# Self-attention on one core: one projection job per head slot, every hand-over between engines one slot later, and the stacked q/k parts moved by group of four heads

## The reference, cut to what matters

```python
def _L0_attn_ref(x, w_qkv, w_out):
    b, s, _ = x.shape
    qkv = (x @ w_qkv).reshape(b, s, 3, HEADS, HEAD_DIM)
    q, k, v = (qkv[:, :, 0], qkv[:, :, 1], qkv[:, :, 2])
    q = q / scale
    scores = jnp.einsum('bqhd,bkhd->bhqk', q, k)
    scores = jnp.where(causal_mask[None, None], scores, NEG)
    attn = jax.nn.softmax(scores, axis=-1)
    out = jnp.einsum('bhqk,bkhd->bqhd', attn, v).reshape(b, s, HIDDEN)
    return out @ w_out
x = x + _L0_attn_ref(_layernorm(x), L0_attn_w_qkv, L0_attn_w_out)
x = x + _L0_xattn_ref(_layernorm(x), ctx_2048, ...)
x = x + _L0_ffn_ref(_layernorm(x), ...)
```

## Time and profile before

| | us |
|---|---|
| median of 3 runs | 863.87 |
| lowest, highest | 860.68, 865.61 |
| profiled execution | 868.03 |
| its span, first to last instruction | 866.3 |
| PE busy in the span | 762.7 |
| DVE, ACT, POOL busy | 529.1, 370.4, 312.2 |

### The profile page before, as it was taken

How to read it: one execution, slowest core, us unless ns; L and a number is a source line. 1 busy time by engine, 2 the same in 40 slices (tenths; PEclk the granted TensorE clock), 3 DMA queues, 4 the chain that set the end, 5 groups by cost and what they waited for, 6 DMA issues and landing times. The chain is left out here.

```text
span 866.3 us, 19948 instructions
## 1 busy us (share of the span) xinstructions
PE 762.7 (88%) x6424; PEld 688.1 (79%) x6425; DVE 529.1 (61%) x1557; ACT 370.4 (43%) x1145; POOL 312.2 (36%) x456
## 2 busy tenths in 40 slices
PE   4798989898989999757999999999999985739995
PEld 4787979888888888646899998989899974637884
DVE  4678685868686867546565655556464533834664
ACT  4476675757575767534423232313133220622221
POOL 3376574757565656641000101010101101124662
PEclk9999999999999999879999999999999997868998
DMA  9643343444444434306712425060502111765630
GB/s 345 147 114 94 105 101 106 93 118 93 116 93 118 93 94 115 101 1 208 286 52 72 99 23 113 8 121 20 101 30 67 59 15 49 168 163 152 199 122 24
DMA packets 49575, 90.90 MB, mean 105 GB/s; under 512 B 11390, under 2 KB 11518, under 8 KB 49408
## 3 DMA queue, kind: packets, MB, share of 16 engines
q1 hardware_dynamic: 43872, 77.80, 34.2%
q0 software_dynamic: 5664, 12.61, 4.7%
HBM read 51.95 MB, written 18.77 MB: 82 GB/s over the span
## 5 line engine op out<-in xcount | busy, mean ns | idle before, releaser
L398 ACT ACTIVATE prob<-prob,nmax 128x128 f32<-128x128 f32 (+1 forms) x256 | 114.5, 448 | 77.9 <-DVE nmax L576 77.9
L337 POOL TENSOR_TENSOR pt_part<-pt_rest,pt_part 128x384 bf16<-128x384 f32 x128 | 117.8, 921 | 10.2
L335 POOL CAST pt_part<-pt_rest 128x384 bf16<-128x384 f32 x128 | 67.4, 527 | 113.5 <-DVE pt_rest L585 112.1
L576 DVE CUSTOM_DVE_ANT_0 prob<-a_s,mask 128x128 f32<-128x128 f32 (+1 forms) x256 | 80.2, 350 | 4.1 <-PE a_s L457 3.2
L585 DVE TENSOR_TENSOR pt_rest<-a_t,pt_part 128x384 f32<-128x384 f32 x128 | 70.8, 553 | 7.2 <-ACT pt_part L408 7.0
L408 ACT CAST pt_part<-a_t 128x384 bf16<-128x384 f32 x128 | 60.6, 473 | 32.3 <-PE a_t L470 32.1
L470 PE MATMUL a_t<-ident,prob 128*128 128x128 f32 x384 | 63.5, 275 | 12.2 <-DVE pt_rest L585 11.8
L457 PE MATMUL a_s<-stack 96*128 96x256 f32 x256 | 61.8, 324 | 0.2 <-DVE nmax L576 0.2
L470 PEld LDWEIGHTS a_t<-ident,prob 128*128 128x128 f32 x384 | 45.2, 141 | 17.9 <-issue 15.3
L488 PE MATMUL a_o<-pt_part,v_part 128*32 128x256 bf16 (+1 forms) x1536 | 40.4, 258 | 14.2 <-POOL pt_part L337 13.9
L922 ACT CAST b_kt_hi<-b_bank 128x256 fp32r<-128x256 f32 (+1 forms) x48 | 20.5, 445 | 66.1 <-PE b_bank L56 65.2
(11 more groups left out here) (217 smaller groups left out, 1986.1 us busy)
## 6 DMA issues: line engine op xcount, KB each, us to landing
stack<-qk SPq DMA_DIRECT2D x192, 128.0 KB, 2.4
stage<-in_w SPq DMA_DIRECT2D x8, 1024.0 KB, 8.9
xin<-in_x SPq DMA_DIRECT2D x8, 512.0 KB, 3.6
xr<-in_x SPq DMA_DIRECT2D x8, 512.0 KB, 3.6
x<-xr SPq DMA_DIRECT2D x8, 512.0 KB, 2.8
xin<-x SPq DMA_DIRECT2D x8, 512.0 KB, 8.9
b_cin<-in_ctx SPq DMA_DIRECT2D x8, 512.0 KB, 3.5
xr<-x SPq DMA_DIRECT2D x8, 512.0 KB
```

The lines of the kernel that those rows point to most:

```text
L335: nc.gpsimd.tensor_copy(pt_part[1][:, t % NPT, :], rest).then_inc(pt_mid_done, 1)
L337: nc.gpsimd.tensor_tensor(pt_part[2][:, t % NPT, :], rest, pt_part[1][:, t % NPT, :], ALU.subtract).then_inc(pt_done, 1)
L398: a = nc.scalar.activation(prob[:, e % NPROB, cols], prob[:, e % NPROB, cols], ACT.Exp, scale=-1.0, bias=nmax[:, e, q:q + 1], accum_out=rs ...
L576: m = nc.vector.tensor_tensor_reduce(out=prob[:, s % NPROB, cols], in0=s_ps[s % 2][:, q, 0:P * (q + 1)], in1=mask[:, P * (1 - q):], scale= ...
```

## The change

**Jobs.** The table has one job in every slot. u0 and u1 are made in their own batch, in slots 2 and 3, and no longer in the prologue and in slots 12 and 13 of the batch before. k3 goes from slot 2 to 1, X0 and X1 from 5 and 6 to 6 and 7, y0 and y1 from 7 and 8 to 8 and 9.

**Hand-overs.** ACT now writes a job's hi part in the slot after the job, as its first work, and DVE writes the lo part in that slot behind the scores of the head. PE does the transposes ahead of the values and the job. On ACT the exponentials go last. The copy of the transposed reciprocals and the copy of the scaled output go one slot later. The norm is stretched: statistics in slot 0, aggregation in 2, reciprocal root in 3, application in 4. `r_sb` and `o_sb` have memory of their own.

**Stack.** It moves by group of four heads: 12 DMAs of 64 KB for each of four groups, each group after its own k job, with one semaphore; PE waits for all 12 at a group's first head.

The diff, cut to what the prediction speaks of:

```diff
-        SLOTS = {0: ["q3"], 2: ["k3"], 4: ["w0"], 5: ["w1", "X0"], 6: ["X1"], 7: ["y0"], 8: ["y1"], 9: ["q0"], 10: ["k0"],
-                 11: ["q1", "k1"], 12: ["u0"], 13: ["u1"], 14: ["q2"], 15: ["k2"]}
+        SLOTS = {0: ["q3"], 1: ["k3"], 2: ["u0"], 3: ["u1"], 4: ["w0"], 5: ["w1"], 6: ["X0"], 7: ["X1"], 8: ["y0"],
+                 9: ["y1"], 10: ["q0"], 11: ["k0"], 12: ["q1"], 13: ["k1"], 14: ["q2"], 15: ["k2"]}
-        PROLOGUE = ["X0", "X1", "q0", "k0", "q1", "k1", "q2", "k2", "u0", "u1"]
+        PROLOGUE = ["X0", "X1", "q0", "k0", "q1", "k1", "q2", "k2"]
-        EPILOGUE_SLOTS = 10
+        EPILOGUE_SLOTS = 11
+        STATS_AT, AGGR_AT, RSTD_AT, APPLY_AT = 0, 2, 3, 4
...
-            def stack_half(half):
+            def stack_group(g, n, early):
+
+                wait(sp, job_ev, job_at(f"k{g}", n) + 1)
+                sp.sem_inc(tick_sp, 1)
+                wait(sp, s_done, early)
                 for j in range(HG):
                     for r, parts in enumerate((slice(0, 3, 2), slice(1, 3), slice(0, 4, 3))):
-                        dst = stack[HD * r:HD * (r + 1), half, j, :, :, :].bitcast(F32)
-                        src = qk[HD * j:HD * (j + 1), half, parts, :, :].bitcast(F32)
-                        sp.dma_start(dst.rearrange("p w g s -> p w (g s)"),
-                                     src.rearrange("p w g s -> p w (g s)")).then_inc(stacked[half][j], 16)
+                        sp.dma_start(stack[HD * r:HD * (r + 1), g, j, :, :].bitcast(F32),
+                                     qk[HD * j:HD * (j + 1), g // GH, parts, g % GH, :].bitcast(F32))\
+                            .then_inc(stacked[g], 16)
...
+                stack_group(2, n - 1, n * H - HG)
...
-                wait(sp, s_done, n * H)
-                stack_half(1)
+                stack_group(3, n, n * H)
...
                 if has("k1", n):
-                    wait(sp, job_ev, job_at("k1", n) + 1)
-                    sp.sem_inc(tick_sp, 1)
-                    wait(sp, s_done, n * H + H // 2)
-                    stack_half(0)
+                    stack_group(0, n, n * H + HG)
+                    stack_group(1, n, n * H + 2 * HG)
...
             def slot(n, h):
+                for j, of in jobs_before(h, n):
+                    if j not in LATE:
+                        evac(j, of)
+                g = group_at(h, ON_LAG, n)
+                if g is not None:
+                    act.wait_ge(r_done, groups_before(h, ON_LAG, n) + 1)
+                    wait(act, on_done, groups_before(h, ON_LAG, n))
+                    nc.scalar.copy(r_sb[:], o_ps[g % 2][:, 1, :]).then_inc(rs_done, 1)
...
-                    if s % (H // 2) < HG:
-                        pe.wait_ge(stacked[g // GH][j], (n + 1) * HEAD_IN)
+                    if j == 0:
+                        pe.wait_ge(stacked[g], (n + 1) * GROUP_IN)
...
-                g = group_at(h, AV_LAG, n)
-                if g is not None:
-                    heads_by_values(g, h, n)
-                for j in jobs_of(h, n):
-                    job(j, n)
                 t = head_at(h, T_LAG, n)
...
+                g = group_at(h, AV_LAG, n)
+                if g is not None:
+                    heads_by_values(g, h, n)
+                for j in jobs_of(h, n):
+                    job(j, n)
...
-                if head_at(h, 0, n) is not None and (not isinstance(n, int) or n < B - 1):
-                    if h == 0:
-                        norm_stats(n + 1)
-                    if h == 2:
-                        norm_apply(n + 1)
+                if norm_at(h, STATS_AT, n):
+                    norm_stats(n + 1)
+                if norm_at(h, AGGR_AT, n):
+                    norm_aggr(n + 1)
+                if norm_at(h, APPLY_AT, n):
+                    norm_apply(n + 1)
```

More of the change, by code:

```diff
@@ L119, in self_attention @@
         job_done, job_hi, job_ev = sem("a_job_done"), sem("a_job_hi"), sem("a_job_ev")
-        stacked = [[sem(f"stacked_{half}_{j}") for j in range(HG)] for half in range(2)]
+        stacked = [sem(f"stacked{g}") for g in range(G)]
         s_done, mx_done, ex_done = sem("s_done"), sem("mx_done"), sem("ex_done")
@@ L179, in jobs_of, with jobs_before, norm_at @@
             return [j for j in SLOTS.get(slot, []) if has(j, n)]
+        def jobs_before(slot, n):
+            t = slot - JOB_LAG
+            if t >= 0:
+                return [(j, n) for j in jobs_of(t, n)]
+            if isinstance(n, int) and n == 0:
+                return []
+            return [(j, n - 1) for j in jobs_of(H + t, n - 1 if isinstance(n, int) else n)]
+        def norm_at(slot, at, n):
+            return slot == at and (not isinstance(n, int) or n < B - 1)
         def head_at(slot, lag, n):
@@ L327, in slot @@
             def slot(n, h):
[L328 removed]
+                if norm_at(h, RSTD_AT, n):
                     next_rstd(n + 1)
@@ L338, in slot @@
                                             ALU.subtract).then_inc(pt_done, 1)
-                before = h - LO_JOB_LAG
-                for j in jobs_of(before, n) if before >= 0 else jobs_of(H + before, n - 1 if isinstance(n, int) else n):
-                    of = n if before >= 0 else n - 1
-                    if j[0] in "uw" and not (isinstance(of, int) and of < 0):
+                for j, of in jobs_before(h, n):
+                    if j[0] in "uw":
                         v_lower_parts(j, of)
@@ L580, in slot @@
                     m.then_inc(mx_done, 1)
+                for j, of in jobs_before(h, n):
+                    if j in LATE:
+                        dve.wait_ge(job_done, job_at(j, of) + 1)
+                        dve.wait_ge(xr_in, 16 * of)
+                        xt = xr[:, int(j[1]), :]
+                        nc.vector.tensor_tensor(xt, bank(j, of)[:, :], xt, ALU.add).then_inc(job_ev, 1)
+                    else:
+                        evac(j, of)
                 t = head_at(h, LO_LAG, n)
```

102 lines of the change are left out of this document (41 added, 61 removed).

## The result

The changed kernel takes 874.33 us (median of 19 runs, 871.2 to 878.09), the kernel before, on the same chip, 866.17 us (19 runs, 860.48 to 871.51). The ratio is 1.0095, with a 95% interval of 1.0078 to 1.0113: it is slower by about 8 us, or 1%. Forecast was 865, that is 1 us more than the 863.87 which the kernel before had then; of the 9.3 us between 865 and 874.33, 2.3 are that the kernel before has a median of 866.17 here.

What follows compares the result with a forecast made beforehand. PE was taken as the bound: 39.2 us of work in a 44.13 us batch, the rest waits. 863.87 + 0 (six steady batches) + 1 (first) + 0.3 (last) = 865 us; 8-in-10 range 855 to 873.

Steps and rivals of the forecast that it cites:

- the gain of 1.7 us a batch by the hand-overs: Steady batch: PE's lost time falls from 4.9 to 3.2 us, as waits for POOL and uncopied jobs go; error 1 us.
- the net of zero for six batches: Steady batches: the hand-overs' gain is given back at the stack, so each stays at 44.1 us.
- waits for DVE at slots 4, 7, 8: PE waits for DVE's `pt_rest` at the transposes of these slots: 0.8, 0.95 and 1.45 us a batch.
- PE's work without waits: Steady batch: the same matmuls as before, so PE's 39.2 us stay.
- the running sum: DVE's work added up against PE's slot starts, 16.4 us in eight slots of 17.3, to place and size PE's waits.
- The stack's wait: Slot 16 (slot 0 of the next batch): PE waits 1.7 to 1.8 us for group 0's twelve DMAs, issued 0.64 apart.
- First batch, +1 forecast: First scores 0.6 us earlier, but v jobs in slots 2 and 3 and a new stack wait: +1, bounds 0 and +4.
- The term for the v jobs: First batch: two v jobs, 2.8 us, leave the prologue for slots 2 and 3, where DVE half hides them.
- Last batch, +0.3 forecast: Its own u0 and u1, 2.8 us, fill slots where PE waits for DVE anyway: +0.3, bounds 0 and +2.8.
- A: Rival: half-size stack DMAs issue in about 0.4 us, so no stack wait; six batches gain 1.7 each, 855 us; chance 0.22.
- C: Rival: the three DVE waits vanish too and only the stack wait remains, 843 us; chance 0.06.
- B: Rival: the clock falls around the X-only slots in all six steady batches instead of one, 872.5 us; chance 0.2.

Runs made afterwards that it cites:

- e1: Changed kernel, but PE waits at each stacked head for its own three DMAs instead of twelve at a group's first head; 859.0 us, ratio 0.9945.
- e9: Changed kernel with waits by head, the norm two batches ahead, and x loaded ahead of the bursts of groups 2 and 3; 866.31 us, ratio 0.9976.
- e11: Changed kernel with waits by head and another job table (both X jobs in slot 8 with values), norm in slots 4, 5 and 7; 845.11 us, ratio 0.9735.
- e2: Changed kernel with u0 and u1 of the first batch alone back in the prologue; 873.63 us, ratio 1.0111.
- e10: Changed kernel with waits by head and u0 and u1 of the last batch left out; 862.1 us, ratio 0.9932.
- e7: Changed kernel with waits by head and PE's jobs ahead of its transposes, as in the kernel before; 866.84 us, ratio 1.0008.

## Why the prediction was wrong

**The step that failed most is the gain of 1.7 us a batch by the hand-overs**, and with it the net of zero for six batches. e1 has the change without the group's wait, and its steady batch is 43.80 us where before has 44.13: 0.3 gained. The stack takes 1.04 (44.84 less 43.80), so a steady batch is 0.7 longer rather than equal. The places of the waits were right, their sizes were not. By the starts in PE's timeline (scores to transposes, less the 0.24 of a slot without a wait), in the forecast's terms:

| a steady batch, us | forecast | measured |
|---|---|---|
| waits for DVE at slots 4, 7, 8 | 0.8, 0.95, 1.45 | 1.05, 1.00, 1.7 |
| small ones at slots 11 and 12 | 0 | 0.45 |
| the stack | 1.7 | 1.1 |
| PE's work without waits | 39.2 | about 39.5 |
| the kernel before: waits, work | 4.9, 39.2 | about 4.7, 39.4 |

e9 and e11 show that the causes of the three waits are those of the running sum: the aggregation in slot 2, and slots that hold only an X job. Slot 4's miss of 0.25 has a reason in the trace. I took 0.58 us for the aggregation in its new place, and it takes 0.86 (213.10 to 213.96), because its last instruction, `a_veps`, takes 0.59 us there (at 213.46), with POOL at work beside it, where before it took 0.17 (at 204.22). Why slot 8's wait is 0.2 longer, and where the small ones come from, stays open. PE's work was nearly the same in both orders, as I had it.

**The stack's wait** was right in its place, its cause and the issue time (0.64 forecast, 0.66 measured). Counted from the start of slot 12 (193.54), group 0 is there after 10.95 us instead of 11.3, since a DMA lands after 2.0 us and not 2.4, and PE is ready for it after 9.9 instead of 9.5: 1.1 instead of 1.7 to 1.8.

**First batch, +1 forecast, +3.0 measured** (the second batch's first scores at 67.45 instead of 64.43). The start is right: 0.6 forecast, 0.8 won (28.48 for 29.26). The wait at slot 16 is 2.1 instead of 1.7. The term for the v jobs had no ground: two leave slots 12 and 13 of this batch as two come into slots 2 and 3, so b0 has as many jobs as before. What makes up the rest isn't in the sum at all: the two falls of the clock, 3 us, where before has none in b0. So b0 is 3.8 longer: 2.1 and 3.0, less 1.3 that the rest gains. e1, which doesn't stand 4.2 us ahead of its first scores, has one of the two falls and starts its second batch at 61.53. That the wait brings the fall fits this, but of the eight waits for the stack over a microsecond in the changed kernel and e2 only four have a fall right behind them, so it is not shown.

**Last batch, +0.3 forecast, +2.5 measured.** No wait for the stack lies in it; I split it ahead of slot 10, in the kernel before, in e1 and in the changed kernel:

```profile
331.77:359.81 28.04, 24.48 (x283) 21.54 (x281) 16.90 (x66) 16.40 (x60) 17.92 (x27) 0.94 0.32 79
359.81:393.72 33.91, 20.66 (x217) 16.21 (x216) 15.79 (x54) 12.73 (x45) 14.60 (x21) 0.80 0.09 32
```
```profile
325.77:355.62 29.85, 27.36 (x304) 24.12 (x303) 16.83 (x68) 18.05 (x64) 18.97 (x30) 0.94 0.39 101
355.62:389.38 33.76, 21.03 (x218) 16.07 (x216) 14.81 (x49) 11.96 (x39) 13.56 (x20) 0.80 0.09 32
```
```profile
340.89:370.37 29.48, 26.97 (x302) 23.75 (x303) 16.55 (x67) 17.48 (x61) 18.14 (x29) 0.94 0.38 98
370.37:405.31 34.94, 24.27 (x217) 18.41 (x216) 14.16 (x49) 12.01 (x39) 13.44 (x20) 0.71 0.09 31
```

Slots 0 to 9 take 1.4 us longer than before (1.8 in e1) at the same granted clock, 0.94, with two jobs more. By e10 the jobs are hidden in this order; but without them its slots get no shorter, since DVE is late, so against the kernel before, which has no such jobs here, their time shows. So the +0.3 was right against this order without the jobs, and not against the kernel before. What sets these slots' length was not varied. Behind slot 10 the changed kernel loses another 1.0, at 0.71 instead of 0.80, and e1 nothing.

**Rivals.** A is refuted by SP's rows. C came to nothing. B did not come where it was expected: from b1 to b6 there are two falls in the kernel before (I had read one) and two now. But the clock has its share, 3 us in b0 and about 1 in the last batch, which I had asked for in the steady batches alone. e7 and e9 show that it can be more.

Together, in the profiled executions: −0.8 at the start, +3.8 in b0, +0.6 in b1, +0.8 in b2, +2.1 in b3 to b5, +2.6 in b6 (0.7 as the others, 1.5 the clock, 0.3 a longer wait for the stack at its end) and +2.5 in the last, 11.6 us. The medians say 8.2. e1 divides it: the wait for a whole group costs about 13 us, and everything else in the change gains about 5.
